# Mixed causal stage: v stationary in four 32-column tiles, turned probabilities moving

## The reference

```python
x = x + _L0_ffn_ref(_layernorm(x, axis=-1), ...)

def _L0_ffn_ref(x, in_proj_w, in_proj_b, out_proj_w, out_proj_b, gate_w, gate_b, expert_w, expert_b, ...):
    q_in = _apply_rope(xh, sin, cos).reshape(B, S, E)
    q = (q_in @ Wq.T + bq); k = (q_in @ Wk.T + bk); v = (x @ Wv.T + bv)     # 16 heads of 16
    scores = jnp.einsum('bqhd,bkhd->bhqk', q, k) * scale
    scores = jnp.where(causal, scores, -inf)
    attn = jax.nn.softmax(scores, axis=-1)
    ctx = jnp.einsum('bhqk,bkhd->bqhd', attn, v).reshape(B, S, E)
    x1 = _layer_norm(x + ctx @ out_proj_w.T + out_proj_b, ln1_w, ln1_b)
    gates = jax.nn.softmax(x1 @ gate_w.T + gate_b, axis=-1)
    ...                                    # the two best experts, their weighted sum, a layer norm
```

## Time and profile before

| | us |
|---|---|
| median of 3 runs | 3781.61 |
| the profiled execution's own time | 3801.12 |
| its span, first to last instruction | 3799.3 |
| mean granted TensorE clock, share of full | 0.967 |
| one pair of the mixed stage, make_v to make_v (1099.93 to 1123.10) | 23.17 |
| one pair of the self stage, make_v to make_v (190.76 to 209.65) | 18.89 |

### The profile page before, as it was taken

One profiled execution on the slowest core, in us unless ns is written; L12 is line 12 of the kernel. 1 busy time (PEld: TensorE's weight loads), 2 busy tenths in 40 slices (PEclk: granted clock), 3 DMA queues, 4 the chain that ended last, 5 costly groups with the idle time before them and its releaser, 6 DMA issues. The chain is left out here.

```text
span 3799.3 us, 71289 instructions
## 1 busy us (share of the span) xinstructions
PE 3555.2 (94%) x25628; PEld 2433.8 (64%) x25629; DVE 1923.6 (51%) x6166; ACT 1630.4 (43%) x3491; POOL 1561.1 (41%) x2142
## 2 busy tenths in 40 slices
PE   8997999998999778999799999999999989999997
PEld 5664555555777664444466666666666658899986
DVE  4664666664777664665454555545555446211123
ACT  4663555554666306777244444444444421111111
POOL 1001333333667515553355555555555547100025
PEclk9999999999999789999999999999999989999998
DMA  9401111100000153000100000000000001799962
GB/s 286 160 0 38 39 38 37 37 13 12 10 18 18 38 174 75 18 18 10 41 7 8 7 7 13 7 7 7 12 7 7 1 5 54 261 324 326 327 218 78
DMA packets 111418, 262.50 MB, mean 69 GB/s; under 512 B 24003, under 2 KB 70240, under 8 KB 95840
## 3 DMA queue, kind: packets, MB, share of 16 engines
q1 hardware_dynamic: 90208, 224.70, 18.3%
q0 software_dynamic: 16384, 26.29, 2.5%
q10 hardware_dynamic: 4608, 8.39, 0.6%
HBM read 196.61 MB, written 62.65 MB: 68 GB/s over the span
## 5 line engine op out<-in xcount | busy, mean ns | idle before, releaser
L2389 POOL TENSOR_SCALAR wide_probs<-wide_probs,wide_inverse 100x361 f32<-100x361 f32 x512 | 607.4, 1199 | 0.1
L2570 ACT ACTIVATE wide_probs<-wide_probs,wide_least 100x361 f32<-100x361 f32 x512 | 300.9, 589 | 627.9 <-DVE wide_least L2636 627.9
L2636 DVE CUSTOM_DVE_ANT_0 wide_probs<-banks,wide_bias 100x361 f32<-100x361 f32 x512 | 251.5, 529 | 124.7 <-issue 124.7
L2387 POOL TENSOR_TENSOR wide_hold_pool<-eps 100x1 f32<-100x1 f32 x256 | 50.9, 199 | 580.1 <-DVE wide_inverse L2642 578.7
L2445 PE MATMUL banks<-w_wide_v,wide_c 64*120 64x512 f32 (+1 forms) x1152 | 263.5, 589 | 2.5 <-DVE wide_v L2622 1.8
L2069 ACT ACTIVATE rot_h<-banks,w_rot_b 128x800 f32<-128x800 f32 x256 | 223.6, 924 | 86.4 <-PE banks L1943 82.9
L2439 PE MATMUL banks<-wide_c,w_wide_k 64*128 64x361 f32 x1536 | 255.4, 464 | 3.1 <-DVE wide_kT L2619 2.3
L2481 PEld LDWEIGHTS banks<-ident,wide_probs 100*120 100x120 f32 (+1 forms) x1536 | 158.8, 172 | 149.7 <-issue 119.3
L2467 PE MATMUL banks<-wide_kT,wide_qT 64*100 64x361 f32 x1024 | 221.7, 510 | 2.3 <-issue 2.2
L3068 ACT ACTIVATE tiles_hT<-banks 128x512 f32<-128x512 f32 x114 | 68.1, 597 | 346.3 <-PE banks L2984 346.3
L2642 DVE RECIPROCAL wide_inverse<-wide_rowsum 100x2 f32<-100x2 f32 x256 | 42.4, 166 | 341.6 <-ACT wide_probs L2570 341.6
(11 more groups left out here) (458 smaller groups left out, 7678.9 us busy)
## 6 DMA issues: line engine op xcount, KB each, us to landing
tiles_w<-in_moe_w SPq DMA_DIRECT2D x114, 1024.0 KB, 5.1
slots<-zeros SPq DMA_DIRECT2D x58, 512.0 KB, 5.6
cross_c<-in_ctxT SPq DMA_DIRECT2D x32, 270.8 KB, 4.3
wide_c<-in_ctxT SPq DMA_DIRECT2D x32, 270.8 KB, 4.1
mix_kT<-slots SPq DMA_DIRECT2D x32, 256.0 KB, 4.1
slots<-mix_kT ACTq DMA_DIRECT2D x32, 256.0 KB, 3.9
tiles_rows<-slots SPq DMA_DIRECT2D x57, 128.0 KB, 4.7
slots<-tiles_out SPq DMA_DIRECT2D x57, 128.0 KB, 4.9
```

The costliest lines, as they stand in the source:

```text
L2389: last = nc.gpsimd.tensor_scalar(t.probs[:, i % RING, j, :], t.probs[:, i % RING, j, :], t.inverse[:, i % RING, j:j + 1], None, ALU.mult)
L2570: last = nc.scalar.activation(t.probs[:, i % RING, j, :], t.probs[:, i % RING, j, :], ACT.Exp, bias=t.least[:, i % RING, j:j + 1], scale=-1.0,
L2636: last = nc.vector.tensor_tensor_reduce(t.probs[:, i % RING, j, :], scores(j), t.bias[:, :], -1.0, LARGEST, ALU.add, ALU.min, t.least[:, i ...
```

## The change

In the mixed stage `by_v` goes and `parts_by_v`, `keep_parts` and `turn_parts` are used as in the self stage. Since no bank is free, the parts lie in columns 400 to 499 of banks 2 and 3, behind the turned probabilities of `turn_probs`; so `parts_by_v` of unit i now waits until `keep_probs` of unit i+1 has read these banks (`turned_last`). The orders of the four engines are changed to match: `turn_parts` of a unit stands behind the `score` three units on, the `divide` of lane 0 moves from the end of an iteration to the start of the next, `gate` moves ahead of the k part, `add(before, 0)` behind `place` and `apply`, and on GpSimd `norm_root(before, 0)` behind the two `rope`.

```diff
-        heads_out = out_bank[0:S, 0:NH * (HD + 1)].rearrange("s (h d) -> s h d", d=HD + 1) if mixture else out_bank[0:S, :].rearrange("s (h d) -> s h d", d=HEAD_ROWS)
-        parts_bank = g.psum[:, 7, 0:ROUNDS * S]
+        heads_out = out_bank[0:S, :].rearrange("s (h d) -> s h d", d=HEAD_ROWS)
+        parts_out = g.psum[:, 2:2 + ROUNDS, BLOCKS * S:BLOCKS * S + S] if mixture else g.psum[:, 7, 0:ROUNDS * S].rearrange("p (r s) -> p r s", r=ROUNDS)
@@ GpSimd, run
-                if before:
-                    norm_root(nc, pool, g, m2, 0, before.lane_n[0])
                 if third:
                     pool.wait_ge(s.yT_ready, after.n)
                     for lane in range(LANES):
                         rope(third, lane)
+                if before:
+                    norm_root(nc, pool, g, m2, 0, before.lane_n[0])
@@ TensorE, parts_by_v
-            def parts_by_v(of, i):
+            def parts_by_v(of, i, turned_last=None):
                 lane, c = i // DC, i % DC
                 pe.wait_ge(a[i].probsT, of.n)
+                if turned_last:
+                    pe.wait_ge(a[(i + 1) % SCORE_UNITS].probsT, turned_last.n)
@@ TensorE, run_mix
                 if here:
                     score(here, 0)
+                if before:
+                    turn_parts(before, 1)
+                    turn_probs(before, 3)
                 if after:
...
                     make_rows(after)
                 if before:
-                    turn_probs(before, 3)
-                    by_v(before, 2)
+                    parts_by_v(before, 2, before)
+                if oldest:
+                    place(oldest)
+                if here:
+                    score(here, 1)
+                if before:
+                    turn_parts(before, 2)
+                if here:
+                    turn_probs(here, 0)
+                if before:
...
                     turn_heads(before, 0, other)
-                if oldest:
-                    place(oldest)
-                if here:
-                    score(here, 1)
-                    turn_probs(here, 0)
-                if before:
-                    project(before, 0)
                 if after:
                     pe.wait_ge(s.yT, after.n)
                     make_part(after, 0, side, s.q_ready)
                 if before:
-                    by_v(before, 3)
+                    parts_by_v(before, 3, here)
+                    project(before, 0)
                 if older:
                     turn_x1(older, oldest)
                 if here:
                     score(here, 2)
+                if before:
+                    turn_parts(before, 3)
+                if here:
                     turn_probs(here, 1)
+                if older:
+                    gate(older)
                 if after:
...
                     make_part(after, 1, other, s.k_ready)
                 if here:
-                    by_v(here, 0)
+                    parts_by_v(here, 0, here)
+                    score(here, 3)
                 if before:
...
                     turn_heads(before, 1, side)
-                if older:
-                    gate(older)
-                if here:
-                    score(here, 3)
+                if here:
+                    turn_parts(here, 0)
                     turn_probs(here, 2)
...
                     make_v(after)
                 if here:
-                    by_v(here, 1)
+                    parts_by_v(here, 1, here)
...
                     project(before, 1)
@@ ScalarE, run_mix: the whole order after the change
+ keep_probs(before, 3)  keep_rows(after)        weigh(here, 0)       keep_parts(before, 2)
+ keep_probs(here, 0)    keep_heads(before, 0)   weigh(here, 1)       keep_q(after)
+ keep_parts(before, 3)  keep_x1(routed)         keep_probs(here, 1)  weigh(here, 2)
+ keep_k(after)          keep_parts(here, 0)     keep_heads(before, 1) keep_probs(here, 2)
+ weigh_gates(routed)    weigh(here, 3)          keep_v(after)        keep_parts(here, 1)
@@ VectorE, run_mix: the whole order after the change
+ shift(here, 0)   divide(before, 0)  first_norm(older, 1)  stats(third)          shift(here, 1)
+ place(oldest)    apply(third)       add(before, 0)        shift(here, 2)        divide(before, 1)
+ first_norm(before, 0)  peak_gates(older)  shift(here, 3)  choose(older)         add(before, 1)
@@ VectorE, start of both stages
-            if not mixture:
-                nc.vector.memset(parts_bank, 0.0).then_inc(s.parts_zero, 1)
+            nc.vector.memset(parts_out, 0.0).then_inc(s.parts_zero, 1)
```

More of the change, by code:

```diff
@@ L140, in causal_phase @@
         s = semaphores(nc, ctx, name, "ones picked k_bias y yT_ready yT q_ready q k_ready k v_ready v rowsum heads headsT_ready headsT proj_ready added parts_zero")
-        a = [semaphores(nc, ctx, f"{name}{i}", "scores_ready masked rowmax shifted probs turned_ready probsT heads_ready parts_ready parts") for i in range(SCORE_UNITS)]
+        a = [semaphores(nc, ctx, f"{name}{i}", "scores_ready rowmax shifted probs turned_ready probsT heads_ready parts_ready parts") for i in range(SCORE_UNITS)]
         t = buffers(nc, ctx, name, y=[S, TURNS, LANES, D], yT=[P, DC, LANES, S], qT=[P, TURNS, DC, LANES, S], kT=[P, TURNS, DC, BLOCKS, LANES, S], v=[S, TURNS, LANES, NH, HD + 1],
@@ L370, in _ @@
             pe.wait_ge(s.ones, 1)
-            if not mixture:
-                pe.wait_ge(s.parts_zero, 1)
+            pe.wait_ge(s.parts_zero, 1)
             if mixture:
@@ L721, in keep_parts @@
                     act.wait_ge(a[i + SCORE_UNITS - PROBS_RING].heads_ready, of.pair)
-                nc.scalar.copy(partsT[:, i % PROBS_RING, :, :], parts_bank.rearrange("p (r s) -> p r s", r=ROUNDS)).then_inc(a[i].parts, 1)
+                nc.scalar.copy(partsT[:, i % PROBS_RING, :, :], parts_out).then_inc(a[i].parts, 1)
             def keep_heads(of, lane, bank):
@@ L778, in run_mix @@
                 routed = older
+                if before:
+                    keep_probs(before, 3)
                 if after:
                     keep_rows(after)
-                if before:
-                    keep_probs(before, 3)
                 if here:
@@ L785, in run_mix @@
                 if before:
+                    keep_parts(before, 2)
+                if here:
+                    keep_probs(here, 0)
+                if before:
                     keep_heads(before, 0, other)
                 if here:
-                    keep_probs(here, 0)
                     weigh(here, 1)
@@ L791, in run_mix @@
                     keep_q(after)
+                if before:
+                    keep_parts(before, 3)
                 if routed:
@@ L798, in run_mix @@
                     keep_k(after)
+                if here:
+                    keep_parts(here, 0)
                 if before:
@@ L808, in run_mix @@
                     keep_v(after)
+                if here:
+                    keep_parts(here, 1)
             runs(act, run_mix if mixture else run_self)
@@ L968, in run_mix @@
                     shift(here, 0)
+                if before:
+                    divide(before, 0)
                 if older:
@@ L974, in run_mix @@
                     shift(here, 1)
-                if before:
-                    add(before, 0)
                 if oldest:
                     place(oldest)
-                if before:
-                    divide(before, 1)
                 if third:
@@ L985, in run_mix @@
                     apply(third)
+                if before:
+                    add(before, 0)
                 if here:
@@ L988, in run_mix @@
                 if before:
+                    divide(before, 1)
                     first_norm(before, 0)
@@ L995, in run_mix @@
                     choose(older)
-                if here:
-                    divide(here, 0)
                 if before:
```

18 lines of the change are left out of this document (2 added, 16 removed).

## The result

The changed kernel takes 3793.18 us, the median of 9 runs (3786.72 to 3802.6), beside 3781.61 of the kernel before, also 9 runs: ratio 1.0035, 95% interval 1.0023 to 1.0046. By the ratio the change costs 13 us where it was to save 17 (forecast 3765); "slower" had a chance of 0.06. Its profiled execution took 3793.18 us (span 3791.3).

The account below looks back on a forecast made before the run. TensorE sets the pace at 23.17 us a pair, VectorE close behind; the new pair, 15.97 + 6.12 = 22.09, saves 1.08. Fourteen pairs (15.1) and the ends (+2) give -17: 3781.6 to 3764.6 us, range 3748 to 3779.

Parts of the forecast that it names:

- What a unit costs: TensorE, per unit: by_v 1.36 us replaced by parts_by_v 0.57 (0.10 for entering) and turn_parts 0.26, saving 0.53.
- rival 4: TensorE drains at both sides of each parts_by_v, adding 1.2 us to the pair's first stretch; 3781 us, chance 0.02.
- stretch A: TensorE from make_v to the start of the k part, three of four units: 17.06 us to become 15.97.
- Stretch B: From the k part's start to the next make_v, set by ScalarE: 6.12 us against 6.11, TensorE idle 1.73.
- rival 3: Clock falls in TensorE's new idle time: in each pair 3789 us, chance 0.06; in some pairs about 3775, chance 0.06.
- What must keep up: VectorE free for shift(here, 2) with slack 0.27 us; GpSimd's later norm_root, some 0.3 late, costs nothing under cover.
- the wait in B: TensorE idle 1.73 us ahead of turn_parts(here, 0) in every pair, until ScalarE's keep_k and keep_parts are done.
- a cover: keep_probs(here, 2), held back over 1 us, delays weigh(here, 3), so shift(here, 3) some 0.3 us late costs nothing.
- the ends: First and last pairs, the drain after and the memset at the stage's start: together +2 us, bounds -3 and +5.
- Rival 2: keep_k on ScalarE still starts late by 0.68 us: pair 22.77, kernel 3774 us; chance 0.17.
- Rival 1: TensorE never waits for keep_parts: pair about 20.4 us, kernel 3741; chance 0.07. Against it: ScalarE's in-order list.

Follow-up runs that it names:

- e10: Kernel after with weigh_gates ahead of keep_probs(here, 2) and one useless 512-column matmul ahead of turn_parts(here, 0): 0.9959 of the kernel before.
- e1: Kernel after with one ScalarE step moved, weigh_gates ahead of keep_probs(here, 2): 1.0020 of the kernel before.
- e5: Kernel after with weigh_gates ahead of keep_probs(here, 2) and two useless matmuls (512, 256 columns) ahead of turn_parts(here, 0): 0.9995 of the kernel before.
- e6: Kernel after with keep_k split, four of eight activations ahead of keep_parts(here, 0), and weigh_gates ahead of keep_probs(here, 2); no filler: 0.9923 of the kernel before.
- e4: Kernel after with two useless matmuls (512 and 256 columns) on TensorE ahead of turn_parts(here, 0): 1.0058 of the kernel before.
- e9: Kernel after with keep_k split, weigh_gates early, norm_root(before, 0) ahead of the ropes, and sixteen useless matmuls behind the last pair: 0.9950 of the kernel before.

## Why the prediction was wrong, point by point

- **What a unit costs.** Right: 0.47 from start to start, 0.26 for turn_parts. Entering the tiles costs no more than the 0.10 charged. The Trainium skill (TensorEngine Tiling (Array Packing), Key Properties) has TensorE drained by the change of mode. Nothing here is as long as rival 4's drain: with 0.25 at both sides of each of its three units stretch A could not be 15.97.
- **Stretch A.** The sum was right where VectorE is in time: 15.97 in e10, with 0.28 of idle time ahead of parts_by_v(before, 2) (0.34 forecast). In the kernel after it is 17.65 at full clock, by VectorE.
- **Stretch B.** Right: 6.24 against 6.12, with 1.58 of the 1.73 idle, ended by keep_parts.
- **Stretch B, its price: the first step that failed.** The wait of 1.73 us was charged as itself and nothing more; the clock was left out of the sum. It was rival 3, with a chance of 0.12 in all. Its mechanism and prices were right (3.4 us at half clock, 1.7 us each; 3789 for a fall in every pair, against 3788.68 of e1, where it did fall in every pair). The evidence set against it, the idle cross stage at full clock, did not carry over, and the narrow by_v, argued to cause the falls and to take them along, are gone while the falls are more. The runs go with the wait: 1.58 us open, a fall in every pair (e1); the wait shortened by a filler (e5, e10) or ended by the split (e6), none in the steady pairs. The Trainium skill (TensorE: Matmul & The Clock Gate, Part 1) says that idleness puts the clock back; these runs agree.
- **What must keep up: the second step that failed.** VectorE's room was worked out for shift(here, 2) and GpSimd's for first_norm, and of ScalarE only the steps that TensorE waits for. I wrote that the wait in B holds keep_probs(here, 2) back by more than 1 us, and took that for a cover. I didn't go on to what is queued behind it: weigh_gates, for which choose waits, with add(before, 1) and shift(here, 0) behind that. It is 30.2 us of VectorE's waiting in 13 pairs, of which 7.3 come back to TensorE.
- **The number of full pairs, and the ends: smaller errors.** 14 pairs at 1.08 were to give 15.1 and the ends +2 (-3 to +5). In e10 the 14 periods from the second to the fifteenth give 11.5: the second is 0.8 longer than before (21.92 against 21.13, with a fall of the clock in it) and the third and fourth gain 0.6 each, because before the change these pairs were shorter than the 23.17 that the sum took for all. The ends give +0.2, inside their bounds, though the first period alone loses 2.0 (17.53 to 19.56) where 0.6 was forecast. So without the two failures the change would have saved some 12 us of the 17.
- **Rival 2** did not come about: keep_k stands ready 0.17 us before the k matmuls end (the idle time ahead of L694, ended by TensorE). Rival 1's reason was sound in both directions: TensorE waited because ScalarE takes its list in order, and once the list was split (e6) the stage fell by 25 us and the kernel by 0.8%, with pairs of 21.3 where the rival had 20.4.

Put together: the new product saves its 2.1 us of TensorE work a pair; about 1 of it was to become idle time. That idle time, in the one place where it stands, made choose late and let the clock fall. In the 13 periods the kernel after takes 25.3 us more than e10. It has 35.6 us at half clock in them, which cost at most half of that, 17.8, and 7.3 us of TensorE's waits on VectorE. The two are not independent: two of the falls, at 1123.6 (6.8 us) and 1198.7, begin at the end of such waits in stretch A, all others at the wait in B. Nor do they add up: with VectorE in time the clock falls in every pair (23.86, e1), with the wait in B filled VectorE's lateness is left with falls of its own (23.79, e4), and both together give 24.14, since in a pair with a fall TensorE comes late enough for VectorE. The 13.2 us of the ratio are 14.9 in the stage, less some 2 from stages that differ between any two executions.

What stays open. In the kernel after the falls end with the one at 1198.7, though the wait of 1.58 us still stands in pairs 13 to 15 (23.28, 23.90 and 23.54 us, with waits on VectorE and no fall), which are idle for 2.6 to 3.3 us in all; e1 falls in every pair with 1.9. So the idle time of a pair doesn't by itself say whether the clock falls. And e4's ratio is some 5 us more (21.9 against before) than its stage (+9.3) and its wide loop (+7.6) explain, which its interval (13 to 31 us) covers.

## What to carry to other kernels

A wait that is forecast on one engine must be followed on, through each thing queued behind it on every engine, until the circle closes or ends in real slack; here the cover for one step was the cause of another's lateness. Idle time on TensorE that recurs once a period can cost more than itself, when the clock goes down after it (here 1.7 us for a wait of 1.58): fill it, or better, split the long step ahead of what TensorE needs. Two causes that hide each other show only when both are taken away; either edit alone looked nearly worthless here. And when a stage gets shorter and the kernel doesn't, look for the difference in stages that weren't touched.

## What was not expected of the hardware

- **Program length moves time in another stage.** Sixteen matmuls more in TensorE's text bring or remove a pause of 1.3 to 1.9 us in six of the seven turns of the wide loop, some 10 us in all, 0.3% of the kernel, as much as the change itself. The pauses wait for nothing that the profile shows. The Trainium skill (Runtime: NRT & Kernel Launch, Instruction fetch mechanics) says that a branch to a target outside the blocks at hand has to fetch it first. The pauses fit this, once a turn (158 us apart) and dependent on position, but no run shows the fetch itself.
- **VectorE beside GpSimd.** The comparison L911 takes 0.29 us in 12 of the 16 pairs of the kernel after and 0.77 to 0.84 in four, among them the pair above; in just these four it runs while GpSimd works on L333 with two operands in SBUF. Three more of choose's steps are stretched alike in the pair above: from L898 to L919 choose takes 4.4 us there and 2.4 at best (3.3 in most pairs before the change). The Trainium skill (SBUF — State Buffer, SBUF: two separate sides) says that such instructions of the two engines shut each other out of a shared port. The times, each about that of one GpSimd instruction (0.73 to 0.86), agree. So a late choose comes out later still when it slides beside the norms on GpSimd.
- **Small matmuls onto one place** take 0.33 us each (5.33 for sixteen of 8 columns, e9), not the 0.12 at most that I had allowed. The single matmul L491 of 16 columns takes 0.18 from its start to the next in the pair of e10. What makes the difference no run shows.
